# A gated block with adapters on one core: GpSimd's gathers set ahead of its subtraction, one load and one group of gathers moved to a later place

## The reference

```
x = x + einsum('bct,bcd->bdt', x, W0[subject])
x = x + einsum('bct,bcd->bdt', x, W1[adapter])
x = x + einsum('bct,bcd->bdt', x, W2[adapter]) + bias[adapter][:, :, None]

def lora_linear(x, W, A, B):                # A, B: 8 adapters of rank 16
    return x @ W + (x @ A[adapter]) @ B[adapter]
gate = lora_linear(x, Wg, Ag, Bg)           # 512 -> 2048
up   = lora_linear(x, Wu, Au, Bu)           # 512 -> 2048
h    = silu(gate) * up
x    = x + lora_linear(h, Wd, Ad, Bd)       # 2048 -> 512
```

## Time and profile before

| | us | note |
|---|---|---|
| median of 3 runs | 1271.38 | 1271.26 to 1272.43 |
| the profiled execution | 1271.38 | its own time |
| its span | 1269.5 | first to last instruction |
| TensorE busy | 1256.2 | 99% |
| TensorE loading weights | 1047.5 | 83%, beside its matmuls |
| VectorE busy | 975.0 | 77% |
| GpSimd busy | 665.8 | 52% |
| ScalarE busy | 552.9 | 44% |

### The profile page before, as it was taken

One profiled execution on the slowest core, in us unless ns is written; L12 is line 12 of the kernel. 1 busy time (PEld: TensorE's weight loads), 2 busy tenths in 40 slices (PEclk: granted clock), 3 DMA queues, 4 the chain that ended last, 5 costly groups with the idle time before them and its releaser, 6 DMA issues.

```text
span 1269.5 us, 17928 instructions
## 1 busy us (share of the span) xinstructions
PE 1256.2 (99%) x6236; PEld 1047.5 (83%) x6236; DVE 975.0 (77%) x1538; ACT 552.9 (44%) x977; POOL 665.8 (52%) x549
## 2 busy tenths in 40 slices
PE   9999999999999999999999999999999999999998
PEld 7778888888888888888888888888888888888886
DVE  7987777887788777788778768878877877777765
ACT  4644445443344454454434444444443443443431
POOL 4466655555635556545654556555554454444462
PEclk9999999999999999999999999999999999999999
DMA  6856345555965344436677445435487632232432
GB/s 198 294 173 218 121 125 158 158 158 166 379 195 181 106 133 139 138 117 175 230 306 211 157 125 151 148 121 145 149 296 258 211 108 82 64 114 100 116 100 100
DMA packets 141047, 210.10 MB, mean 165 GB/s; under 512 B 43424, under 2 KB 87712, under 8 KB 140960
## 3 DMA queue, kind: packets, MB, share of 16 engines
q1 hardware_dynamic: 118656, 138.07, 35.1%
q0 software_dynamic: 22016, 70.80, 16.6%
q10 hardware_dynamic: 288, 0.10, 0.0%
HBM read 164.89 MB, written 44.04 MB: 165 GB/s over the span
## 4 chain that ended last, share of the span: by engine, by line
PE 88%; DVE 5%; DMA 3%; issue 2%; POOL 1%; ACT 0%; SPq 0%; DVEq 0%; ACTq 0%; POOLq 0%
PE px L1522 27%; PE pd L1522 26%; PE py L1522 13%; PE pz L1522 6%; PE pz L1539 3%; PE pv L1586 2%; PE pv L1583 2%; PE pd L1779 2%; PE py L1539 2%; PE px L1539 2%; PE pd L1622 1%; DMA w_raw<-w_gu 1%; PE pd L1549 1%; DVE wg_lo L1197 1%; DMA b_got<-b_table,idx_b 1%
## 5 line engine op out<-in xcount | busy, mean ns | idle before, releaser
L689 POOL TENSOR_TENSOR h_lo<-g,h_hi 128x512 fp32r<-128x512 f32 x127 | 184.4, 1452 | 333.7 <-ACT h_hi L807 333.0
L658 POOL DMA_INDIRECT b_got<-b_table,idx_b x192 | 199.0, 1036 | 59.5 <-issue 51.4
L1522 PE MATMUL px<-xo_hi,wg_hi 128*128 128x512 f32 x540 | 216.9, 402 | 3.6 <-ACT up L807 1.9
L1329 DVE TENSOR_TENSOR acc<-pd,acc 128x512 f32<-128x512 f32 x252 | 168.0, 686 | 64.9 <-PE pd L1522 63.7
L1197 DVE TENSOR_TENSOR wg_lo<-w_raw,wg_hi 128x512 fp32r<-128x512 f32 (+1 forms) x268 | 192.6, 721 | 31.9 <-issue 19.0
L1522 PE MATMUL px<-xo_hi,wg_lo 128*128 128x512 f32 x540 | 211.8, 392 | 0.0
L1522 PE MATMUL px<-xo_lo,wg_hi 128*128 128x512 f32 x540 | 210.3, 389 | 0.0
L807 ACT ACTIVATE wg_hi<-w_raw 128x512 fp32r<-128x512 f32 (+1 forms) x272 | 152.7, 570 | 117.8 <-PE py L1539 73.4
L1522 PE MATMUL pd<-wd_hi,h_hi 128*128 128x512 f32 x512 | 202.8, 396 | 0.0
L1522 PE MATMUL pd<-wd_lo,h_hi 128*128 128x512 f32 x512 | 201.0, 393 | 0.0
L1522 PE MATMUL pd<-wd_hi,h_lo 128*128 128x512 f32 x512 | 199.8, 390 | 0.0
(11 more groups left out here) (290 smaller groups left out, 2406.8 us busy)
## 6 DMA issues: line engine op xcount, KB each, us to landing
w_raw<-w_gu SPq DMA_DIRECT2D x68, 512.0 KB
wd_raw<-w_dn SPq DMA_DIRECT2D x64, 256.0 KB
xo_hi<-xops SPq DMA_DIRECT2D x21, 512.0 KB, 6.0
xo_lo<-xops SPq DMA_DIRECT2D x21, 512.0 KB, 7.0
acc<-x SPq DMA_DIRECT2D x8, 1024.0 KB, 8.9
ad_raw<-ad_table SPq DMA_DIRECT2D x16, 512.0 KB
out<-acc SPq DMA_DIRECT2D x7, 1024.0 KB, 5.2
xops<-st_hi SPq DMA_DIRECT2D x24, 256.0 KB, 2.7
```

Of the source, the lines that this page charges most:

```text
L658: gp.indirect_dma_start(out=dst, out_offset=None, in_=rows_of, in_offset=bass.IndirectOffsetOnAxis(ap=rows.bitcast(U32), axis=0)).then_inc ...
L689: return gp.tensor_tensor(dst, src_raw, src_hi, ALU.subtract)
L1329: ins = dve.tensor_tensor(dst, pd[j][:, :], dst, ALU.add)
L1522: ins = pe.matmul(psum, w_parts[wi], x_parts[xi], start=(start and i == 0), stop=(stop and i == 2), skip_group_check=more)
```

## The change

Three things are moved, and no computation is added or taken away.

1. On SyncE `load_ad` stands behind the work on a piece instead of ahead of it.
2. On GpSimd the three gathers into the first half of `b_got` stand ahead of `h_low(q, b, 0)`.
3. On GpSimd `gather_bd(3, 0)` moves from b = 14 to the end of b = 15, ahead of `gather_bd(3, 1)`.

```
@@ SyncE, in the loop over units
-                if b >= 0 and b % AD_BLOCKS == 0 and n > 1:
-                    load_ad(q, b // AD_BLOCKS)
                 k = piece_at(q, b)
                 if k is not None and n:
...
                     store_b(k)
+                if b >= 0 and b % AD_BLOCKS == 0 and n > 1:
+                    load_ad(q, b // AD_BLOCKS)
@@ GpSimd, in the loop over units
-                if (q, b) != (0, 0):
-                    h_low(q, b, 0)
                 if gathers:
                     gp.wait_ge(*piece_out(max(0, m - 1)))
                     gp.wait_ge(p3_mm, n)
                     gather_b(to_q, m, 0)
+                if (q, b) != (0, 0):
+                    h_low(q, b, 0)
                 if b == BLOCKS - 2 and q + 1 < QUARTERS:
                     for g in range(2, AD_GROUPS):
                         gather_ad(q + 1, g)
-                if b == BLOCKS - 2 and q + 1 == QUARTERS:
-                    gp.wait_ge(bdown_mm, q * QP)
-                    gather_bd(q, 0)
...
-                if b == BLOCKS - 1 and q + 1 < QUARTERS:
+                if b == BLOCKS - 1:
                     if q == 0:
                         gp.wait_ge(bd_out, 2 * 16)
                     else:
                         gp.wait_ge(bdown_mm, q * QP)
 
-                    gp.wait_ge(xops_out[0], TP * (q + 1) * 64)
+                    gp.wait_ge(xops_out[0], TP * min(q + 1, QUARTERS - 1) * 64)
                     gather_bd(q, 0)
-                elif b == BLOCKS - 1:
-                    gp.wait_ge(p4_mm, n)
-                    gather_bd(q, 1)
+                    if q + 1 == QUARTERS:
+                        gp.wait_ge(p4_mm, n)
+                        gather_bd(q, 1)
```

## The result

The changed kernel takes 1291.98 us (median of 4 runs, 1290.88 to 1294.22), the kernel before 1271.41 (1271.26 to 1272.43): a ratio of 1.0163, 95% interval 1.0145 to 1.018. The forecast was 1293. The profiled execution of after took 1289.79 us, its span is 1288.0; against the profiled execution of before (span 1269.5) that is +18.5. The medians differ by 20.6, some 2 us more. The profiled execution of after was quicker than all four that were timed (1290.88 at the least) and the others left no trace, so where these 2 us lie isn't shown.

The account below looks back on a forecast made before the run. TensorE, busy 1256.2 of 1269.5 us, was taken to bound the kernel. 16.7 + 2.5 - 1.7 + 2.95 + 0.9 = 21.4 us on 1271.38 gave 1292.8, said as 1293; own range 1284 to 1300, widened to 1277 to 1301.

Parts of the forecast that it names:

- Place 1: Gathers ahead of h_low in 31 odd units: h_low ends late, TensorE waits 0.54 us in each, 16.7 us together.
- both starts: First gather 0.27 us behind p3_mm, or half a microsecond later; either way the third ends at about 495.9.
- The b = 1 term: In the four units with b = 1, VectorE's sums also hold the gathers and h_low: 2.5 us more together.
- What comes back: GpSimd's second trio and second h_low end earlier; TensorE's wait at 83 us and some small ones go: -1.7 us.
- Place 2: load_ad behind the pieces at (0, 4): ad_raw lands at 138.0 and TensorE loses 2.95 us once (bounds 0.2 to 4.3).
- Place 3: gather_bd(3, 0) at the end: TensorE waits 1.4 us, partly absorbed by queued stores, +0.9 us (bounds 0 to 2).
- Rival A: The gathers just fit, the third not held by gate 1; 0.02 us per odd unit, +4.3: 1275.7 us; chance 0.12.
- Rival B: More is held: each trio meets two VectorE operations, or delayed sums hold back weights; +33: 1304 us; chance 0.09.
- C: Faster: gathers fit, load and tail covered, if h_low ends by 496.7 and ad_raw lands by 134.4; 1269.3 us; chance 0.05.

Follow-up runs that it names:

- exchanged waits: The kernel after with the two waits ahead of the first gather in the other order, p3_mm named first: 1289.29 us, 1.0149 of before.
- late gate: The kernel after with those two waits in the other order and, on VectorE, weights_low(n + 1, 3) ahead of gate1(): 1274.04 us, 1.0028 of before.
- moved bd gathers: The kernel before with only gather_bd(3, 0) moved behind the last h_low, run twice: 1275.42 us (1.0027) the first time, 1270.06 us (0.9999) the second.

## Why the prediction was right

**Place 1.** The mechanism was right in each link, both starts included, and the size nearly: 0.54 predicted, 0.58 measured. The start of the half was right (5.7 behind `p3_mm` predicted, 5.61 measured); TensorE starts 0.05 behind `h_low` where I had put 0.15, so that the wait itself came out 0.45, and I had left out the 0.11 us of the first matmul after a stall. The two errors nearly cancel. The b = 1 term (2.5 on top) was too large: the four lost 3.5 in all, 1.2 more than four ordinary ones. With (2, 5) and (3, 9) the odd units sum to 20.0, against my 16.7 + 2.5 = 19.2.

**What comes back** was under-sized: 3.9 in this pair of traces, some 2.8 of it by the change, instead of 1.7. The wait at 83 us was named, with 1.3 instead of 1.45; of the small ones I counted 0.4 where four had 0.34 to 0.59. My list of waits began with the longest group and I stopped there.

**Place 2** was 2.2 instead of 2.95. The failing number is the 3.4 us that I put between the last store's landing and the load's; it was 2.3 (134.7 to 137.0).

**Place 3** was 1.3 at the last pair, as forecast (1.4), but none of it reaches the end, which hangs on the large store issued ahead of it: 0 instead of +0.9.

Together +18.5 in the profiled execution, where the sum said 21.4. That the medians differ by 20.6 is nearer to the forecast than its terms deserve, and that is luck: 2 us of it are in no wait that a trace shows, and the errors of the terms lie on both sides. Rival A failed in both kernels, for two different reasons: in after the first gather starts 0.48 us later than A needs, and with the exchanged waits gate 1 holds the third gather, by 0.05 us. The late gate shows that A would have been right with both out of the way: the gathers then just fit. Rival B would have needed two holds per trio; only the unit (0, 1) shows two long gathers (1.33 and 1.14). C fails on both its conditions (`h_low` ends 5.56 behind `p3_mm` where 5.0 was the limit, `ad_raw` lands at 137.0).

The Trainium skill (SBUF — State Buffer, "SBUF: two separate sides") calls the port pair a lock held for a whole instruction by whichever starts first. In before it fits: `h_low` of 493.98 started ahead of gate 1 and held it, and this operation of VectorE started ahead of `h_low`, kept its usual length and left `h_low` with 1.61 us:

```profile
493.76 0.68 DVE L1197 TENSOR_TENSOR wg_lo<-w_raw,wg_hi 128x512 fp32r<-128x512 f32 x1
```

In the late gate it doesn't: gate 1 started at 496.30, ahead of the `h_low` of 496.68, and it was gate 1 that was held, in all 27 units. Where the page and these rows differ, the rows decide: starting first did not protect VectorE there. Gate 1 had started inside the third gather (495.71 to 496.66); whether that is what made the difference, no run tests. The prediction also spoke of the rule as if it covered gathers; the page states it for an operation of VectorE with two inputs in SBUF only against a GpSimd operation that reads SBUF, and what gathers do is shown by the rows below alone.

## What to carry to other kernels

An idle stretch of a helper engine is cover only up to the moment at which its next result is wanted: measure from the event that opens it to the consumer's start (here 5.16 us), and add up what you put there, start and gaps included. Below that point work is free, beyond it each unit pays one for one: two gathers cost nothing, three 0.58 us, a further 1.34 us of work 1.34. When two engines meet within hundredths, work out both branches; here they had a common end, one set by the late start, the other by VectorE's operation. And compare traces piece by piece: between two single executions 1.6 to 4.2 us can lie in the start, as in three of these traces, and another microsecond in small waits that one trace has and the next has not.

## What the runs showed of the hardware

- A gather that carries the wait on TensorE itself starts 0.27 or 0.28 us after the matmul's end (30 of the 31 units with the exchanged waits); with that wait in an instruction ahead of it, 0.75 to 0.77 (29 of the 31 units of after).
- A gather is held by a VectorE operation only if that runs when the gather starts and has both inputs in SBUF. In the fourteen traces, from 70 us on, 906 gathers took more than 1.05 us; such an operation was running at the start of each, and each ended 0.81 to 0.85 us behind it. The 977 gathers that started beside an idle VectorE took at most 0.97, also where operations started inside them, and none of those that started beside an operation that reads PSUM was long.
- VectorE's gate 1 overlapped by GpSimd's subtraction ends 0.55 or 0.56 us behind it, whichever of the two started first (before: 496.14 against 495.59; late gate: 498.53 against 497.97).
- The semaphores that TensorE raises can rise late and close together. In the first trace with the moved bd gathers the last products ended (by their modelled ends) at 1264.15, 1264.83, 1265.51 and 1266.18, and their semaphore rose at 1266.33, 1266.38, 1266.43 and 1266.48; VectorE, which wanted the first, started then. What held the signals is open.

```profile
1266.36 0.69 DVE L1346 TENSOR_TENSOR acc<-px,acc 128x512 f32<-128x512 f32 x1 [2.80 <-PE pv L1619]
```

- The start of the program varies: at 70 us the other traces are between 0.6 us ahead of before and 4.2 behind it. In the first trace with the moved bd gathers VectorE stood 3.9 us for something the trace calls remote, TensorE waited 1.9 us for it, and behind that wait, from 18 to 22 us, its granted clock was 0.50, the lower of its two levels (1.2 GHz; before, 1.00 there). What VectorE stood for is open. The stretches of that trace (us, busy time of each engine, then the granted clock, DMA share, GB/s):

```profile
12.00:18.00 6.00, 4.06 (x33) 3.95 (x33) 2.08 (x4) 1.33 (x4) 3.80 (x5) 0.83 0.73 236
18.00:22.00 4.00, 4.00 (x21) 4.00 (x21) 2.22 (x6) 0.00 (x0) 0.00 (x0) 0.50 0.38 129
```
